# First relational sum of a graph network: 11 of 750 row gathers become row-by-row transfers issued by SyncE

## The reference, cut to what matters

```
W = einsum('rb,bio->rio', comp, V)         # 8 relations
H = einsum('ni,rio->nro', x, W)            # 3125 x 8 rows of 128
m = H[src, etypes] * norm                  # one row of H for each edge, times its weight
agg = segment_sum(m, dst, num_segments=N)  # rows added up by destination
h = relu(agg + bias)
```

## Time and profile before

| | us |
|---|---|
| median of 3 runs (lowest, highest) | 7113.91 (7109.94, 7127.44) |
| span of the profiled execution, first to last instruction | 5490.5 |
| median less that span | 1623.4 |
| first and last gather of the stage start | 1227.5, 2195.8 |
| last product of the stage ends | 2213.8 |

### The profile page before, as it was taken

One profiled execution on the slowest core, in us unless ns is written; L12 is line 12 of the kernel. 1 busy time (PEld: TensorE's weight loads), 2 busy tenths in 40 slices (PEclk: granted clock), 3 DMA queues, 4 the chain that ended last, 5 costly groups with the idle time before them and its releaser, 6 DMA issues. The chain is left out here.

```text
span 5490.5 us, 78448 instructions
## 1 busy us (share of the span) xinstructions
PE 3904.0 (71%) x20888; PEld 3086.8 (56%) x20888; DVE 2868.1 (52%) x9305; ACT 2397.6 (44%) x5139; POOL 3864.0 (70%) x3978
## 2 busy tenths in 40 slices
PE   3888888767443333797777776676666667988885
PEld 2666666734443333487777764665665554555554
DVE  3677777767432222564444456777777763332222
ACT  3655655322000000353333345665566627766662
POOL 6777777627777777677777757777777716777773
PEclk7888888679575655897878789999999978999997
DMA  5444444333122222522222227665555502222221
GB/s 132 117 113 114 117 112 117 111 139 96 47 55 52 53 52 52 167 63 59 61 60 60 60 63 202 167 162 158 158 158 157 157 13 78 62 60 59 59 58 41
DMA packets 410665, 524.37 MB, mean 96 GB/s; under 512 B 102841, under 2 KB 295013, under 8 KB 409853
## 3 DMA queue, kind: packets, MB, share of 16 engines
q0 software_dynamic: 126592, 262.15, 19.0%
q1 hardware_dynamic: 280956, 256.84, 15.6%
q10 hardware_dynamic: 2689, 0.36, 0.1%
HBM read 469.69 MB, written 49.28 MB: 95 GB/s over the span
## 5 line engine op out<-in xcount | busy, mean ns | idle before, releaser
L1899 POOL DMA_INDIRECT arena<-tab_x,idx_a x880 | 838.1, 952 | 319.4 <-issue 265.2
L804 POOL DMA_INDIRECT arena<-tab,idx_a x784 | 777.7, 992 | 244.8 <-issue 236.8
L1208 POOL DMA_INDIRECT arena<-tab_rel,idx_b x750 | 740.9, 988 | 233.1 <-issue 228.2
L546 POOL DMA_INDIRECT arena<-tab_rel,idx_b x758 | 735.8, 971 | 238.8 <-issue 220.7
L1310 POOL DMA_INDIRECT arena<-tab_h,idx_a x686 | 663.6, 967 | 270.3 <-issue 208.7
L1255 PE MATMUL PS<-arena,att 128*128 x1664 | 351.0, 398 | 520.4 <-DMA arena<-tab_rel,idx_b 514.5
L1255 PEld LDWEIGHTS PS<-arena,att 128*128 128x128 f32 x1664 | 326.9, 302 | 544.1 <-issue 544.0
L1401 PE MATMUL PS<-arena,H 128*128 128x512 f32 x1200 | 541.8, 606 | 11.5 <-ACT arena L1347 11.5
L1229 DVE TENSOR_SCALAR att<-iota_row,drel,wgt 128x128 f32<-128x128 f32 x832 | 221.8, 366 | 572.7 <-PE PS L1255 572.7
L662 DVE TENSOR_TENSOR arena<-arena,PS 128x128 f32 x832 | 240.9, 290 | 492.6 <-PE PS L619 402.1
L615 PE MATMUL PS<-arena,att 128*128 x1664 | 343.7, 343 | 165.9 <-POOLq L552 132.1
(11 more groups left out here) (420 smaller groups left out, 8371.2 us busy)
## 6 DMA issues: line engine op xcount, KB each, us to landing
arena<-pair_d SPq DMA_DIRECT2D x220, 256.0 KB
arena<-tab_u SPq DMA_DIRECT2D x880, 64.0 KB
arena<-drel_rows SPq DMA_DIRECT2D x104, 512.0 KB
tab_rel<-arena SPq DMA_DIRECT2D x50, 512.0 KB
arena<-tab_rel,idx_b POOLq DMA_INDIRECT x1508, 2.5
arena<-tab_x,idx_a POOLq DMA_INDIRECT x880
arena<-tab,idx_a POOLq DMA_INDIRECT x784
arena<-tab_h,idx_a POOLq DMA_INDIRECT x686
```

What stands on the lines that cost most here:

```text
L546: pool.indirect_dma_start(out=G[:, o:o + D], out_offset=None, in_=table, in_offset=bass.IndirectOffsetOnAxis(ap=idx_row[:, c:c + 1], axis= ...
L804: pool.indirect_dma_start(out=G[:, o:o + 136], out_offset=None, in_=tab0, in_offset=bass.IndirectOffsetOnAxis(ap=idx_src[:, 8 * s + k:8 * ...
L1208: pool.indirect_dma_start(out=G[:, o:o + D], out_offset=None, in_=table, in_offset=bass.IndirectOffsetOnAxis(ap=idx_row[:, c:c + 1], axis= ...
L1899: pool.indirect_dma_start(out=self.G[:, o:o + D], out_offset=None, in_=tab_x, in_offset=bass.IndirectOffsetOnAxis(ap=idx_pair[:, 4 * g + u ...
```

## The change

In 11 of the 98 groups (11, 19, 27, and so on to 91) GpSimd gathers 7 blocks in place of 8. The eighth block of each is fetched by SyncE, with 128 transfers of one row each, which read their row number from SBUF into a register and take it as the place in the table. For that SyncE first writes the row numbers of the 11 blocks to device memory (`by_row`, one transfer that turns columns into rows) and loads them back as 11 rows on one partition. In groups from 16 on it waits for the ring as GpSimd does. TensorE waits for one more semaphore in those 11 groups. The store of `aside.stores` moves behind six of the blocks on SyncE's queue.

```diff
@@ build
+        by_row = dram("by_row", [11, P], I32)
@@ stage_sum
-            s_first, s_pos, m_done, sum_done = (sem(name + x) for x in ("_first", "_pos", "_m", "_s"))
+            s_first, s_pos, m_done, sum_done, s_ix = (sem(name + x) for x in ("_first", "_pos", "_m", "_s", "_ix"))
+            ROWS = [g for g in range(11, GROUPS_N) if g % 8 == 3]
+            assert len(ROWS) == 11
+            s_rows = [sem(f"{name}_rows{q}") for q in range(4)]
+            row_ix = [idx_a[0:1, 128 * i:128 * (i + 1)] if i < 6 else
+                      extra[0:1, 192 + 128 * (i - 6):320 + 128 * (i - 6)].bitcast(I32) for i in range(11)]
+
+            def gathered(g):
+
+                return 7 if g in ROWS else min(8, 2 * ST - 8 * g)
+
+            def landed_count(s):
+
+                return 16 * sum(8 if g < plain.GROUPS else gathered(g) for g in range(s % RG, s + 1, RG))
             with nc.Block() as block:
                 @block.sync
                 def _(sp):
                     sp.dma_start(v3(first), bias.unsqueeze(0).unsqueeze(0).to_broadcast([P, 4, D])).then_inc(s_first, 16)
                     aside.loads(sp)
-                    aside.stores(sp)
+                    sp.dma_start(by_row.rearrange("g e -> e g"), idx_row[:, 8 * ROWS[0] + 7:2 * ST:64],
+                                 allow_slow_non_contiguous=True).then_inc(s_ix, 16)
+                    sp.wait_ge(s_ix, 16)
+                    for i in range(11):
+                        sp.dma_start(row_ix[i], by_row[i:i + 1, :]).then_inc(s_ix, 16)
+                    sp.wait_ge(s_ix, 192)
+                    for i, g in enumerate(ROWS):
+                        if i == 6:
+                            aside.stores(sp)
+                        if g >= RG:
+                            sp.wait_ge(sum_done, g - RG + 7)
+                        o = (8 * g + 7) % (8 * RG) * D
+                        for e in range(0, P, 4):
+                            _, rows = nc.values_load_multi_w_load_instructions(
+                                row_ix[i][0:1, e:e + 4], engines=[mybir.EngineType.SP], min_val=0,
+                                max_val=NP * R_REL - 1,
+                                skip_runtime_bounds_check_because="node numbers and edge types are in range, as for the gathers")
+                            for u, r in enumerate(rows):
+                                sp.dma_start(G[e + u:e + u + 1, o:o + D], table[bass.ds(r, 1), :]
+                                             ).then_inc(s_rows[i % 4], 16)
@@ gpsimd
-                        for c in range(8 * g, min(8 * g + 8, 2 * ST)):
+                        for c in range(8 * g, 8 * g + gathered(g)):
@@ tensor
-                            pe.wait_ge(full[s % RG], 128 * (s // RG) + 16 * min(8, 2 * ST - 8 * s))
+                            pe.wait_ge(full[s % RG], landed_count(s))
+                        if s in ROWS:
+                            i = ROWS.index(s)
+                            pe.wait_ge(s_rows[i % 4], 16 * P * (i // 4 + 1))
```

## The result

| | us |
|---|---|
| median before, 4 runs (lowest, highest) | 7111.92 (7093.43, 7127.44) |
| median after, 4 runs (lowest, highest) | 7510.69 (7507.07, 7513.56) |
| ratio, 95% interval | 1.056 (1.0545 to 1.0576) |
| predicted | 7100.1, range 7090 to 7155 |

The account below looks back on a forecast made before the run. GpSimd's 750 gathers were taken to bound the stage; eleven fewer save 13.8 us, SyncE's rows staying covered and 1623.4 us outside the span unchanged: 7113.9 - 13.8 = 7100.1 us, range 7090 to 7155.

Parts of the forecast that it names:

- The price of a row: SyncE's queue in the stage: 0.30 us frame plus 0.25 issue, 0.55 a row, 70.4 a block, 774 for all.
- the 1623.4 us carried over unchanged: Whole kernel: median 7113.91 us against a span of 5490.5; the difference lies outside the trace and stays as it is.
- The third rival: Outside the span: time there grows by 20.7 ns for each added SyncE instruction, +95 us, kernel 7195 us; chance 0.04.
- I cost the transport at nothing: Queue behind SyncE: it keeps up at twice the bytes and more, so moving the rows adds 0 us.
- 22,500 reckoned: Queue behind SyncE: the small packets expected from the row transfers, beside which gathers might take 1 to 2% longer.
- Does GpSimd itself slow down? I take nothing.: GpSimd's gathers beside SyncE's transfers: no slowdown assumed; 2% of 739 gathers would be 14 us.
- The cover is 17 us here, and grows.: First row block at the ring: 17 us to spare; GpSimd asks per 79.3 us, SyncE needs 70.4.
- the start: SyncE's first row, behind the edge attributes, turned row numbers and eleven loads: at about 1302 us, stage starting at 1227.5.
- The first rival: SyncE's queue becomes the bound, GpSimd waits for `sum_done`; decides from 0.614 us a row; 7266 us; chance 0.23.
- Its formula: End of SyncE's path in the stage: 1335 + 1408 r us for a row of r us.
- 11 x 1.258 = 13.8 us: GpSimd in the steady part of the stage: eleven gathers fewer at 1.258 us each save 13.8 us.

Follow-up runs that it names:

- e0_before_again: The kernel before, unchanged, profiled once more: 7086.99 us.
- e1_static_rows: Kernel after, its 1408 row transfers issued from places fixed in the program, without register loads or address arithmetic: 7092.61 us.
- e4_no_gathers: Kernel after, GpSimd's gathers of this stage left out from group 5 on, rows still fetched and waited for: 6819.34 us.
- e9_eleven_left_out: Kernel after, with nobody fetching or waiting for the rows of the eleven left-out gathers: 7105.31 us, ratio 0.9976 to the kernel before.
- e3_two_queues: Kernel after, rows 0 to 63 of each block issued by SyncE, 64 to 127 by ScalarE's queue: 7192.71 us, ratio 1.0103.
- e11_store_later: Kernel before with four blocks fetched early by SyncE into own buffers, moved behind the next block's rows, small store after the third: 7119.56 us, ratio 1.0008.

## Why the prediction was wrong

Two steps failed. The price of a row, 0.55 us where 1.016 were measured, carries the 399 us: it was taken from places where nothing was held. The one ahead of it, the 1623.4 us carried over unchanged, left the sum near the time before, but hid that in the timed executions instructions are held.

**"1623.4 us lie outside of what the trace shows. I carry them over unchanged."** They lie inside the span of the executions that were timed: in e0_before_again 457 us of them ahead of the stage (first gather at 1684.9, not 1227.5), 176 in it and the rest behind it. The difference of 30% between a span and the median was the largest number of the case, and it was read as an offset though nothing in the profile showed one. The third rival took it up, as a price per instruction outside of the span; the runs show instead 1.7 us around the span and instructions held within it. The earlier trace rows made the stage GpSimd's alone; in a timed execution TensorE is held so often that it is nearly as late, and GpSimd waits 181.2 us at the ring.

**"A row then costs 0.30 + 0.25 = 0.55 us, a block 70.4, all of them 774."** Right in itself: an issue takes 0.225 us in the median (0.25 predicted), and without gathers a row takes 0.571, all of them 804.1 us. Wrong for the place where it runs: 1.016 on average. The durations of the earlier trace rows came from an execution in which hardly anything was held. The Trainium skill, page "DMA: Bandwidth & Descriptors", in the table inside "Why a DMA increments its semaphore by 16 and not by 1", gives 512 cycles for a plain transfer on earlier generations, the prediction's estimate of 0.427 us; the trace doesn't agree, with its 0.225.

**"I cost the transport at nothing"** held, as e1_static_rows shows. The packets were overcounted: beside 22,500 reckoned, queue q1 has 285218 - 280956 = 4262 more of them in the kernel after, by its page.

**"Does GpSimd itself slow down? I take nothing."** It doesn't: 955 ns in the median against 952. But the question was asked in one direction only. What the gathers do to SyncE was left out, and e1_static_rows and e4_no_gathers put the loss there. With the two prices that the runs give, 2.11 us beside gathers with no long stop and 0.571 with GpSimd standing, the kernel after can be estimated: for each block GpSimd has 63 gathers, 79.3 us, beside which SyncE gets out 79.3 / 2.11 = 38 rows; for the other 90 it stands, 90 x 0.571 = 51 us; together 130.7 us. Measured: 1430.0 / 11 = 130.0. In e0_before_again eight groups took (2818.1 - 1684.9 - 73.2) / 94 x 8 = 90.2 us, so ten periods cost 10 x (130.0 - 90.2) = 398 us. The same sum gives 79.3 + 26 x 0.571 = 94 us for half blocks (97.3 measured). That it comes out so near is in part luck. The seventh block of the kernel after, up to where GpSimd stops:

```profile
2604.71 88.80 SPq L1225 DMA_DIRECT2D arena<-tab_rel  x61
```

Sixty-one rows, not 38, come out before the stop, in 90 us with two short ones in them, and 67 in the 44.1 us that GpSimd stands. The fifth to the tenth block are alike (55 to 66 rows before, 62 to 73 in the stop); the other five took from 107 to 154 us as a whole. The long first stop of 76.5 us, which the kernel before has too, isn't in the sum.

**"The cover is 17 us here, and grows."** It shrank with each block, since SyncE needed 130 us where GpSimd's gathers take 79. Also the start was late: the first row came 97.1 us after the first gather, not 75. The issue that turns the row numbers:

```profile
1721.10 31.29 SPq L1207 DMA_DIRECT2D by_row<-idx_b  x1
```

The turned numbers were there 80 us after the first gather (68 reckoned), and the eleven loads behind them took 12 us, not 3. e1_static_rows starts 94 us behind the first gather as well and loses nothing, so this term decided nothing.

**The first rival** had the place and the way: SyncE's queue, GpSimd waiting for `sum_done`. Its formula, with the measured r of 1.016, gives 1335 - 1227.5 + 1430 = 1538 us for the stage, and 1554.8 were measured; most of the difference is the start, which came 22 us later. Its mechanism was wrong: it made the issue dear (0.367 to 0.628), while the issue is the cheapest of all and the holding beside gathers makes the row dear. The dearest of its prices gave 7542, near the 7510.69 by chance.

**"11 x 1.258 = 13.8 us"**: borne out by e9_eleven_left_out, 17 us (9 to 26). The Trainium skill, "Perfetto Trace Analysis", DMA Optimizations, says that where descriptor generation is the bottleneck, balancing DMAs over the engines that can issue them may help. That is what this change does, and the runs show no gain from it here (ratio 1.056). What they show is the price: one gather of 128 rows occupies GpSimd for 1.26 us, 0.01 a row; SyncE needs 0.57 at best for one row.

## What to carry to other kernels

Price an instruction stream beside the engine that will be busy with it, not in a quiet place, and ask for both directions who slows whom. Where span and timed median differ by 30%, find out where the difference lies before anything is added to it. Work that one queue gives to another must be early, not only fast on average: measure how long before its due time the buffer is free, and look at which waits stand ahead of it on the queue.

## What the runs showed of the hardware that was not expected

- Beside GpSimd's gathers issued back to back, instructions of TensorE and SyncE come at a pace of multiples of 0.70 us, and ScalarE's issues last up to 1568 ns (e3_two_queues): the starts of TensorE's products in e0_before_again are 2.80, 2.10 and 2.80 us apart, where they are 0.20 apart in a pause of GpSimd. SyncE shows the same (single issues of up to 1398 ns, and of at most 293 without gathers). In the stretch shown it ends some 4 us after the gathers stop, and sets in again some 6 us after they go on; in e11_store_later it grows while they last (nine rows in the first half of the 30 us shown, four in the second). Through what part of the chip they are held, and whether by the issuing of the gathers or by their transfers, no run here shows.
- What is held seems to be each instruction, not each byte or transfer: rows of one instruction (e1_static_rows) took 0.73 us each and came in time, rows with a run-time address took 1.016 and didn't, and register operations that move no row lasted up to 1395 ns (51 without gathers).
- One profiled execution of the kernel before had none of this beside the same gathers (208 products in 25.18 us) and a span of 5490.5 us; all its other executions, timed and profiled, took from 7087 to 7142. What made it so is open.
- The queue took the 1408 transfers of 512 bytes, each to one partition, without a wait that counts: in e1_static_rows TensorE waited 13.3 us for them in all.
